# Cross-attention in two-step cycles of four runs on TensorE, PSUM banks in three pairs, exponential in two instructions

## The chip, the cores and the metric

The kernel runs on one core of a Trainium2 chip. The metric is device time in microseconds (us) of one execution, launch to end, as the median of several runs. Engines: PE is TensorE (matmul), ACT is ScalarE, DVE is VectorE, POOL is GpSimd, SP is SyncE, which here only issues DMAs. They run side by side, each in its own program order, and wait for each other by semaphores.

## The reference, cut to what matters

A decoder layer on x of shape (32, 56, 256): multi-query self-attention, then cross-attention to a context of shape (32, 1500, 256) with a mask, then a feed-forward part with quantised inputs and weights. The change touches the part after the self-attention:

```python
q = proj(layernorm(x), Wq, bq, 56)                     # 16 heads of 16
k = proj(ctx, Wk, bk, 1500); v = proj(ctx, Wv, bv, 1500)
scores = clip(q k^T / 4, -50, 50); scores = where(mask, scores, -50)
probs = softmax(scores)                                 # over 1500
x = x + layernorm(clip(rs, 0, .3) * ((probs v) Wo^T + bo)) * g + b
h = silu(bitlin(layernorm(x), gate_w)) * bitlin(layernorm(x), val_w)
x = x + bitlin(h, out_w)      # bitlin rounds its input to 127 steps of the row's maximum
```

## The kernel before, in words

The first block (up to about 349 us) does the self-attention; the change doesn't touch it. The second, `block_b`, does the rest and takes the batches in 16 pairs (i = 0 to 15). A batch's context is 1500 columns, loaded in three chunks of 500, so a pair has six chunks (c = 0 to 5), numbered x = 6i + c over the whole kernel. A chunk is four tiles of 125; two tiles are a twin, so a pair has 12 twins (t = 0 to 11), of which the first six are the first batch's.

What the engines do for it, with the four kinds of PE work by the letters that the text uses:

- SP loads chunk x + 3 into a ring of three buffers `raw` once POOL has read the one before it (line 1094).
- ACT copies it to `high` (fp32r, `split_high`, line 1199) and POOL subtracts to get `low` (`split_low`, line 1140), one instruction for each 128 rows, so two each.
- PE projects keys in two pieces, `piece` 0 and 1 (**K**, line 1451, 6 matmuls of 128x500 each), and values in two, `piece` 2 and 3 (**V**, line 1460, 12 matmuls of 128x256 each). All use the whole array. A piece goes to one of two PSUM banks `proj_ps[0]` and `proj_ps[1]`; keys are read out by ACT (`keys_out`, line 1204), values by DVE (`values_copy`, line 1251).
- PE makes the scores of a twin (**S**, line 1478): 16 fp32 matmuls (32 instructions) that use 32 rows of the array each, in four row groups; group r writes bank r of `score_ps`. ACT takes the exponential of all four banks in one instruction (`exp_twin`, line 1212), DVE limits and masks it in place, one instruction for each of the twin's two tiles (`limit`, line 1260).
- PE adds up probabilities times values and ones (**A**, `add_up`, line 1503): 32 fp32 matmuls (64 instructions) that use 32 columns of the array each, into `sum_ps`. After six twins DVE reads the sums (`read_sums`) and divides (`divide`).

The rest of the layer for pair i - 1, the tail, is spread over pair i by step numbers 0 to 12, one for each twin: two divides, 2 `project` (PE line 1520, then statistics on DVE), 3 `add_delta` (waits for POOL's `power`, line 1164, an inverse square root), 4 `quantise_rows`, 5 `rows_turned`, 6 and 7 the gate products and `gates`, 8 and 9 the value products, `values_` and `silu`, 10 `quantise_hidden`, 11 `hidden_turned`, 12 `finish`. The tail's products go through one bank, `side_ps`, guarded by `side_ready` and `side_read`.

With the four banks of `score_ps`, two of `proj_ps`, `sum_ps` and `side_ps` all eight PSUM banks are taken.

The order is written out by hand, one `body` for each engine. PE's repeats for each twin t: S(t), then K (t even) or V (t odd) of the next chunk, then A(t - 1). S(t) waits for the exponential of t - 1 (the four banks are free), K waits for the value copies and V for the key copies of the same bank, A waits for both `limit` of its twin. `exps` has two buffers. ACT: exponential of t, then for even t `keys_out` and `split_high` by turns. DVE: two `limit` of t - 1, then the tail step, and for odd t two `values_copy`. POOL, for each chunk c: two `split_low` (they wait for the two `split_high` of ACT), and behind them, in chunk 1, the two `power` and `add_bias` of the tail (lines 1166 to 1180). At the end of the kernel the tail of the last pair runs by itself, with idle matmuls (`spare`, line 907) between its steps.

Of the kernel before, what the change touches and what calls it, by code (L numbers as in the profile page):

```python
# [26 lines left out]
P = 128  # L27
# [34 lines left out]
GATES = (7, 8)  # L62
AFTER = (2, 5)
# [922 lines left out]
def block_b(nc, dram, out, keep, early):  # L986
# [3 lines left out]
    with ctx:  # L990
# [21 lines left out]
        exps = [sb(f"exps{n}", [TILE, 2, HR, QW]) for n in range(2)]  # L1012
# [26 lines left out]
        score_ps = ctx.enter_context(nc.psum_tensor("score_ps", [P, HR, 512], F32))  # L1039
        proj_ps = [ctx.enter_context(nc.psum_tensor(f"proj_ps{n}", [P, 512], F32)) for n in range(2)]  # L1040
# [43 lines left out]
        def up_ps(p, n):  # L1084

            return score_ps[0:ROWS, n - 2, :] if p == LAST else side_ps[0:ROWS, :]
# [108 lines left out]
        def _(act):  # L1195
# [5 lines left out]
            def keys_out(x, p, r):  # L1201

                act.wait_ge(piece_ready, 4 * x + p + 1)
                nc.scalar.activation(keys[r][:, p, :], proj_ps[p][:, 0:CHUNK], ACT.Identity,  # L1204
                                     bias=b_k[:, p:p + 1]).then_inc(keys_ready, 1)

            def exp_twin(i, t, warm):

                act.wait_ge(scores_ready, NT * i + t + 1)
                if warm:  # L1210
                    act.wait_ge(probs_used, NT * i + t - 1)
                nc.scalar.activation(exps[t % 2][:, :, :, :].rearrange("p h r n -> p r h n"),  # L1212
                                     score_ps[0:TILE, :, 0:2 * QW].rearrange("p r (h n) -> p r h n", h=2),
                                     ACT.Exp, scale=0.25).then_inc(exps_ready, 1)
# [6 lines left out]
            def body(i, first, last):  # L1221
                for t in range(NT):
                    c, half = divmod(t, 2)
                    x = PC * i + c
                    exp_twin(i, t, not first or t >= 2)
                    if half == 0:
                        for p in range(DC):
                            if not (last and c == PC - 1):
                                keys_out(x + 1, p, (c + 1) % 2)
                            if not (last and c >= PC - 2):  # L1230
                                split_high((c + 2) % 3, 2 * i + (c + 2) // 3 + 1, c % 2, p)
                    if not first and t in GATES:
                        gate_tanh(i - 1, GATES.index(t))

# [12 lines left out]
        def _(dve):  # L1247

            def values_copy(x, q, r):
                dve.wait_ge(piece_ready, 4 * x + q + 3)  # L1250
                nc.vector.tensor_copy(vals[r][:, 2 * q:2 * q + 2, :, 0:HD],  # L1251
                                      proj_ps[q][0:TILE, :].rearrange("p (k h d) -> p k h d", k=2, d=HD))\
                  .then_inc(vals_ready, 1)

            def limit(i, t, half):

                dve.wait_ge(exps_ready, NT * i + t + 1)
                tile = exps[t % 2][:, half, :, :].rearrange("p r n -> p (r n)")
# [135 lines left out]

            TAIL = 2 + 1 + 2 + 2 + 3 + 1 + 2 + 2 + 4 + 3 + 1 + 1

            def body(i, first, last):
                tail = {} if first else tail_steps(i - 1, False)
                for t in range(NT):
                    c, half = divmod(t, 2)  # L1400
                    for k in range(2):
                        if t:
                            limit(i, t - 1, k)
                        elif not first:
                            limit(i - 1, NT - 1, k)
                    if t == 1 and not first:
                        read_sums(i - 1, 1)
                    if t == BN + 1:
                        read_sums(i, 0)
                    if t in tail and t not in AFTER:  # L1410
                        tail[t]()
                    if last and t == BN + 3:
                        divide(i, 0)
                    for q in range(2) if half == 1 and not (last and c == PC - 1) else ():
                        if q == 1 and t in tail and t in AFTER:
                            tail[t]()
                        values_copy(PC * i + c + 1, q, (c + 1) % 2)
# [252 lines left out]
```

## Time and profile before

| | |
|---|---|
| median of 3 runs (lowest, highest) | 1390.54 us (1390.42, 1393.0) |
| the profiled execution | 1393.26 us, its span 1391.5 us |
| busy PE, PE weight load | 1369.0, 1171.2 us |
| busy DVE, ACT, POOL | 997.8, 720.7, 518.4 us |
| granted PE clock | 0.998 of full speed |

The span is from the first to the last instruction. Busy time is the union of an engine's instructions. A matmul's end is modelled, and the matmuls overlap in the array, so a PE that is busy all the time may still lose time between them: the distance between the starts of two matmuls is what shows it. In the views a group of like instructions is merged into one row: its start, the time from the first start to the last end, and its count.

### The profile page before, as it was taken

Reading aid. Unit: us, or ns where it says so; the run is one execution under the profiler, and the core shown is the slowest. Engines: PE = TensorE matmul, PEld = TensorE weight load, DVE = VectorE, ACT = ScalarE, POOL = GpSimd, SP = SyncE. Lnnn points to the kernel's source line nnn. Section 1 sums busy time; section 2 is a strip of 40 time slices with the busy share of each in tenths; the row PEclk is TensorE's granted clock in tenths of the full one; section 3 lists DMA queues with packets and bytes.
Section 4 is the critical chain, followed back from the end, with each engine's and each line's share of the span. In section 5 each row is a group of like instructions: output and inputs, shape, how many; then the busy total and the mean of one; then the engine's idle time right before and its main releaser. Section 6 shows DMA issues by size and latency. Waiting matters only on the chain.

```text
span 1391.5 us, 55868 instructions
## 1 busy us (share of the span) xinstructions
PE 1369.0 (98%) x25409; PEld 1171.2 (84%) x25409; DVE 997.8 (72%) x1821; ACT 720.7 (52%) x943; POOL 518.4 (37%) x494
## 2 busy tenths in 40 slices
PE   8999999999999999999999999999999999999997
PEld 6788888886888888888888888888888888888884
DVE  5788788785356867777676867677776868677766
ACT  3555454543555555555555555555554555555550
POOL 4656666651324233333323332433333242333310
PEclk9999999999999999999999999999999999999999
DMA  7010001010411211121202121121212122111100
GB/s 193 1 36 2 31 1 32 2 52 1 129 52 48 64 48 50 47 65 33 70 31 78 51 62 50 47 64 33 65 32 80 33 64 65 48 51 47 51 3 8
DMA packets 38957, 66.81 MB, mean 48 GB/s; under 512 B 3749, under 2 KB 36962, under 8 KB 38722
## 3 DMA queue, kind: packets, MB, share of 16 engines
q1 hardware_dynamic: 38722, 63.24, 15.4%
q8 instruction: 201, 3.29, 1.0%
q14 instruction: 34, 0.28, 0.1%
HBM read 61.40 MB, written 1.84 MB: 45 GB/s over the span
## 4 chain that ended last, share of the span: by engine, by line
PE 72%; DVE 2%; issue 0%; POOL 0%; DVEq 0%
PE proj_ps L1460 20%; PE proj_ps L1451 20%; PE score_ps L1478 15%; PE sum_ps L1503 13%; PE side_ps L1538 2%; PE side_ps L1552 1%; PE side_ps L1520 1%; PE side_ps L1545 1%; DVE amax L1338 0%; DVE hidden L1360 0%; DVE sig L1370 0%; DVE hidden L1371 0%; PE side_ps L1527 0%; DVE exps L1260 0%; DVE totals L1282 0%
## 5 line engine op out<-in xcount | busy, mean ns | idle before, releaser
L1212 ACT ACTIVATE exps<-score_ps 125x1792 f32<-125x1792 f32 x192 | 320.8, 1671 | 430.7 <-PE score_ps L1478 430.7
L1260 DVE TENSOR_SCALAR exps<-exps,top 125x896 f32<-125x896 f32 x384 | 289.0, 795 | 21.8 <-ACT exps L1212 17.5
L1478 PE MATMUL score_ps<-spread,keys 32*125 32x112 f32 x6144 | 219.0, 279 | 0.0
L1251 DVE COPY vals<-proj_ps 125x512 f32<-125x512 f32 x192 | 129.5, 688 | 115.6 <-PE proj_ps L1460 113.3
L1503 PEld LDWEIGHTS sum_ps<-exps,vals 125*32 125x32 f32 x12288 | 163.0, 110 | 47.1 <-issue 34.2
L1478 PEld LDWEIGHTS score_ps<-spread,keys 32*125 32x125 f32 x6144 | 184.8, 183 | 15.4 <-issue 0.3
L1503 PE MATMUL sum_ps<-exps,vals 125*32 125x56 f32 x12288 | 191.5, 215 | 0.0
L1140 POOL TENSOR_TENSOR low<-raw_early,high 128x500 fp32r<-128x500 f32 x64 | 84.4, 1323 | 217.8 <-PE proj_ps L1451 217.1
L1140 POOL TENSOR_TENSOR low_early<-raw_early,high_early 128x500 fp32r<-128x500 f32 x62 | 90.3, 1475 | 167.7 <-PE proj_ps L1451 167.7
L1204 ACT ACTIVATE keys<-proj_ps,b_k 128x500 f32<-128x500 f32 x192 | 130.0, 677 | 23.6 <-PE proj_ps L1451 19.8
L326 POOL TENSOR_TENSOR swapped<-swapped,sin 128x448 f32<-128x448 f32 (+1 forms) x72 | 85.6, 1192 | 79.4 <-ACT swapped L597 78.5
L737 PE MATMUL unit_ps<-xnT,w_q 128*128 128x224 f32 x512 | 107.8, 356 | 2.4 <-issue 1.8
L737 PEld LDWEIGHTS unit_ps<-xnT,w_q 128*128 128x128 f32 x512 | 92.6, 190 | 3.9 <-issue 2.1
L1140 POOL TENSOR_TENSOR low_early<-raw,high_early 128x500 fp32r<-128x500 f32 x32 | 40.6, 1274 | 129.1 <-PE proj_ps L1451 129.1
L1140 POOL TENSOR_TENSOR low<-raw,high 128x500 fp32r<-128x500 f32 x32 | 40.1, 1254 | 121.8 <-issue 113.7
L1460 PE MATMUL proj_ps<-w_h,high 128*125 128x256 f32 x384 | 82.7, 296 | 0.0
L1460 PE MATMUL proj_ps<-w_h,high_early 128*125 128x256 f32 x384 | 82.1, 295 | 0.0
L340 POOL TENSOR_TENSOR qT<-qT,swapped 128x448 f32<-128x448 f32 x56 | 76.5, 1376 | 2.2
L596 ACT COPY swapped<-unit_ps 64x448 f32<-64x448 f32 (+1 forms) x72 | 36.7, 510 | 77.5 <-PE unit_ps L737 59.5
L1460 PE MATMUL proj_ps<-w_l,high 128*125 128x256 f32 x384 | 76.7, 281 | 0.0
L1460 PE MATMUL proj_ps<-w_h,low 128*125 128x256 f32 x384 | 76.6, 281 | 0.0
L1460 PE MATMUL proj_ps<-w_h,low_early 128*125 128x256 f32 x384 | 76.5, 280 | 0.0
(186 smaller groups left out, 2742.7 us busy)
## 6 DMA issues: line engine op xcount, KB each, us to landing
raw_early<-in_ctxT SPq DMA_DIRECT2D x64, 500.0 KB, 4.1
raw<-in_ctxT SPq DMA_DIRECT2D x32, 500.0 KB, 3.5
w_q<-in_attn_Wq SPq DMA_DIRECT2D x4, 512.0 KB, 8.5
out<-y_out SPq DMA_DIRECT2D x16, 112.0 KB, 2.3
rows<-in_x SPq DMA_DIRECT2D x1, 1344.0 KB, 17.8
raw_early<-in_attn_Wo SPq DMA_DIRECT2D x1, 1024.0 KB, 18.0
raw_early<-in_ffn_gate_wT SPq DMA_DIRECT2D x1, 1024.0 KB, 5.3
raw_early<-in_ffn_val_wT SPq DMA_DIRECT2D x1, 1024.0 KB, 4.9
```

What stands on the lines that cost most here:

```text
L326: nc.gpsimd.tensor_tensor(swapped[r % 4][:, 0:w].rearrange("p (n s) -> p n s", s=S), swapped[r % 4][:, 0:w].rearrange("p (n s) -> p n s", ...
L340: nc.gpsimd.tensor_tensor(dst, dst, swapped[r % 4][:, :].rearrange("p (h b s) -> p h b s", h=2, s=S), ALU.add).then_inc(turned_ready, 1)
L737: ins = nc.tensor.matmul(to[:, h * GR:(h + 1) * GR].rearrange("p (b s) -> p b s", s=S), w_q[:, c, at:at + DH], xnT[g % 2][:, c, :, 0:S], s ...
L1140: nc.gpsimd.tensor_tensor(low[r][:, k, :], raw[ring][:, k, :], high[r][:, k, :].bitcast(F32), ALU.subtract).then_inc(low_ready, 1)
L1204: nc.scalar.activation(keys[r][:, p, :], proj_ps[p][:, 0:CHUNK], ACT.Identity, bias=b_k[:, p:p + 1]).then_inc(keys_ready, 1)
L1212: nc.scalar.activation(exps[t % 2][:, :, :, :].rearrange("p h r n -> p r h n"), score_ps[0:TILE, :, 0:2 * QW].rearrange("p r (h n) -> p r ...
L1251: nc.vector.tensor_copy(vals[r][:, 2 * q:2 * q + 2, :, 0:HD], proj_ps[q][0:TILE, :].rearrange("p (k h d) -> p k h d", k=2, d=HD))\
L1260: nc.vector.tensor_scalar(tile, tile, LIMIT_LO, top[:, n, at:at + 1], ALU.max, ALU.min)\
L1451: ins = nc.tensor.matmul(proj_ps[p][:, 0:CHUNK], w[:, 0, k, p * P:(p + 1) * P], part[r][:, k, :], start=(n == 0 and k == 0), stop=(n == 2 ...
L1460: ins = nc.tensor.matmul(proj_ps[p - 2][0:TILE, q * D:(q + 1) * D], part[r][:, k, at:at + TILE], w[:, 1, k, :], start=(n == 0 and k == 0), ...
L1478: ins = nc.tensor.matmul(score_ps[0:TILE, r, to:to + HE * S], keys[c % 2][32 * r:32 * r + 32, k, (at + half) * TILE:(at + half + 1) * TILE ...
L1503: ins = nc.tensor.matmul(sum_ps[32 * h:32 * h + VW, g, :], value_and_ones(c % 2, at + half, HJ * g + h), exps[t % 2][:, half, r, col:col + S],
```

## The change

Only `block_b` changes.

- PSUM: instead of four banks for scores and two for pieces there are three pairs of banks: `strip_ps` (two banks, scores of row groups 2 and 3 always) and `pair_ps[0]`, `pair_ps[1]`, which take turns: one holds the scores of row groups 0 and 1, the other the pieces.
- The exponential of a twin is two instructions of half the size: first over `strip_ps`, then over the pair. `exps_ready` counts both. `exps` has three buffers.
- PE's order is written for cycles m = 0 to 5 of a pair, with the even twin e = 2m and the odd one o = 2m + 1: S(e), A(e - 2), A(e - 1), S(o), tail step e, K, tail step o, V. So every kind of work follows itself twice.
- S(o) waits for the first half of the exponential of e, and for both value copies of the chunk (`vals_ready`), since its pair held the pieces of the cycle before. The next S(e) waits for both halves of the exponential of o. K waits for both halves of e's.
- ACT: exponential of e, of o, and then both `keys_out` and `split_high`. The two tanh of the tail move to m = 3 and m = 4.
- DVE: two `limit` of e, tail step e, two `limit` of o, tail step o, two `values_copy`. The tail steps 0 and 10 stand ahead of the `limit` of e.
- POOL and SP are unchanged.

```diff
+TWINS = NT // 2
+SLOTS = 3
-        score_ps = ...psum_tensor("score_ps", [P, HR, 512], F32)
-        proj_ps = [...psum_tensor(f"proj_ps{n}", [P, 512], F32) for n in range(2)]
+        strip_ps = ...psum_tensor("strip_ps", [P, HR // 2, 512], F32)
+        pair_ps = [...psum_tensor(f"pair_ps{n}", [P, 2, 512], F32) for n in range(2)]
+        def score_bank(t, r):
+            return pair_ps[(t // 2 + t) % 2][0:TILE, r, :] if r < HR // 2 else strip_ps[0:TILE, r - HR // 2, :]
+        def piece_bank(x, p):
+            return pair_ps[(x + 1) % 2][:, p % 2, :]
...
 exp_twin(i, t, warm):
                 act.wait_ge(scores_ready, NT * i + t + 1)
                 if warm:
-                    act.wait_ge(probs_used, NT * i + t - 1)
-                nc.scalar.activation(exps[t % 2]..., score_ps[0:TILE, :, 0:2 * QW]..., ACT.Exp, scale=0.25)
-                    .then_inc(exps_ready, 1)
+                    act.wait_ge(probs_used, NT * i + t - SLOTS + 1)
+                for at, banks in ((HR // 2, strip_ps), (0, pair_ps[(t // 2 + t) % 2])):
+                    nc.scalar.activation(exps[t % SLOTS][:, :, at:at + HR // 2, :]..., banks[0:TILE, :, 0:2 * QW]...,
+                        ACT.Exp, scale=0.25).then_inc(exps_ready, 1)
 ACT body:
+                for m in range(TWINS):
+                    exp_twin(i, 2 * m, ...)
+                    if not first and m == 4:
+                        gate_tanh(i - 1, 1)
+                    exp_twin(i, 2 * m + 1, ...)
+                    for p in range(DC):
+                        keys_out(x + 1, p, (m + 1) % 2)
+                        split_high((m + 2) % 3, ..., m % 2, p)
+                    if not first and m == 3:
+                        gate_tanh(i - 1, 0)
 DVE body:
+            AHEAD = (0, 10)
+                for m in range(TWINS):
+                    e, o = 2 * m, 2 * m + 1
+                    if e in AHEAD and e in tail:
+                        tail[e]()
+                    for k in range(2):
+                        limit(i, e, k)
+                    if e == 0 and not first:
+                        read_sums(i - 1, 1)
+                    if e == BN:
+                        read_sums(i, 0)
+                    if e in tail and e not in AHEAD:
+                        tail[e]()
+                    for k in range(2):
+                        limit(i, o, k)
+                    if o in tail:
+                        tail[o]()
+                    for q in range(2) if not (last and m == PC - 1) else ():
+                        values_copy(PC * i + m + 1, q, (m + 1) % 2)
 piece(x, p, r):
-                    pe.wait_ge(vals_ready, 2 * x + p - 1)
+                    pe.wait_ge(exps_ready, 2 * (2 * x - 1))
 scores(i, t):
-                if warm:
-                    pe.wait_ge(exps_ready, NT * i + t)
+                if t % 2:
+                    pe.wait_ge(exps_ready, 2 * (NT * i + t) - 1)
+                    pe.wait_ge(vals_ready, 2 * (PC * i + c) + 2)
+                elif warm:
+                    pe.wait_ge(exps_ready, 2 * (NT * i + t))
 PE body:
+                for m in range(TWINS):
+                    e, o = 2 * m, 2 * m + 1
+                    scores(i, e, not first or e >= 1)
+                    for n in (e - 2, e - 1):
+                        add_up(i, n, ...)          # of pair i - 1 where n < 0
+                    scores(i, o)
+                    if e in tail:
+                        tail[e]()
+                    piece(x, 0, r); piece(x, 1, r)
+                    if o in tail:
+                        tail[o]()
+                    piece(x, 2, r); piece(x, 3, r)
+                    # the last cycle: no pieces, but
+                    #   pe.wait_ge(exps_ready, 2 * (NT * PAIRS - 1)); spare(3); add_up(i, e, True)
+                    if o == NT - 1 and not first:
+                        tail[NT]()
```

## Rows read from the trace of the kernel before

**Rows 1.** The page: busy us of each engine, share of the span, instructions.

```profile
PE 1369.0 (98%) x25409; PEld 1171.2 (84%) x25409; DVE 997.8 (72%) x1821; ACT 720.7 (52%) x943; POOL 518.4 (37%) x494
```

**Rows 2.** PE, timeline: start, us, operation. A, S (then V), A, project, A.

```profile
923.37 0.99 PE L1503 MATMUL sum_ps<-exps,vals 125*32 125x56 f32 x64
924.30 1.14 PE L1478 MATMUL score_ps<-spread,keys 32*125 32x112 f32 x32
...
928.40 0.99 PE L1503 MATMUL sum_ps<-exps,vals 125*32 125x56 f32 x64
...
933.21 1.03 PE L1520 MATMUL side_ps<-w_xo,heads 128*112 128x256 f32 x4
...
934.17 0.99 PE L1503 MATMUL sum_ps<-exps,vals 125*32 125x56 f32 x64
```

**Rows 3.** PE, what is left of the A group of 923.37 in two later windows.

```profile
923.59 0.77 PE L1503 MATMUL sum_ps<-exps,vals 125*32 125x56 f32 x48
...
923.79 0.58 PE L1503 MATMUL sum_ps<-exps,vals 125*32 125x56 f32 x32
```

**Rows 4.** PE where the block starts: first matmuls of K, V, S, K, S.

```profile
348.92 0.69 PE L1451 MATMUL proj_ps<-high_early,w_h 128*128 128x500 f32 x2 [0.30 <-PEq L108]
...
351.72 0.40 PE L1460 MATMUL proj_ps<-w_h,high_early 128*125 128x256 f32 x2
...
354.64 1.14 PE L1478 MATMUL score_ps<-spread,keys 32*125 32x112 f32 x32
355.71 0.72 PE L1451 MATMUL proj_ps<-high,w_h 128*128 128x500 f32 x2
...
358.62 1.14 PE L1478 MATMUL score_ps<-spread,keys 32*125 32x112 f32 x32
```

**Rows 5.** ACT: two lines (fastest/median/slowest ns), then timeline after the S of 354.64.

```profile
L1212 ACT ACTIVATE exps<-score_ps x192: 1665/1671/1677, 355.8 to 1355.7; 125x1792 f32<-125x1792 f32 x192
...
L1218 ACT ACTIVATE sig<-gate x32: 619/628/634, 452.1 to 1378.2; 112x512 f32<-112x512 f32 x32
...
355.85 1.67 ACT L1212 ACTIVATE exps<-score_ps 125x1792 f32<-125x1792 f32 x1 [3.25 <-PE score_ps L1478]
...
358.73 0.68 ACT L1204 ACTIVATE keys<-proj_ps,b_k 128x500 f32<-128x500 f32 x1
```

**Rows 6.** The power line (fastest/median/slowest ns), then timeline about one: ACT, POOL, DVE.

```profile
L1164 POOL TENSOR_TENSOR rstd_b<-var_eps_b,minus_half_b x32: 582/655/1170, 429.8 to 1372.8; 112x1 f32<-112x1 f32 x32
...
932.65 0.61 ACT L1199 CAST high<-raw_early 128x500 fp32r<-128x500 f32 x1
...
933.39 2.53 POOL L1140 TENSOR_TENSOR low<-raw_early,high 128x500 fp32r<-128x500 f32 x2 [6.72 <-PE proj_ps L1451]
...
937.43 0.48 DVE L1314 SCALAR_TENSOR_TENSOR x<-delta,rstd_b,rows 112x256 f32<-112x256 f32 x1
...
939.41 1.28 DVE L1251 COPY vals<-proj_ps 125x512 f32<-125x512 f32 x2
```

**Rows 7.** DVE against POOL: two lines (fastest/median/slowest ns), then one meeting in the timeline.

```profile
L1260 DVE TENSOR_SCALAR exps<-exps,top x384: 673/681/1685, 357.5 to 1362.2; 125x896 f32<-125x896 f32 x192
...
L477 DVE TENSOR_TENSOR probs<-probs,sums x16: 1092/1829/1835, 41.8 to 328.5; 128x896 f32<-128x896 f32 x16
...
965.54 1.68 DVE L1260 TENSOR_SCALAR exps<-exps,top 125x896 f32<-125x896 f32 x1
...
965.25 1.48 POOL L1140 TENSOR_TENSOR low_early<-raw_early,high_early 128x500 fp32r<-128x500 f32 x1 [6.75 <-PE proj_ps L1451]
```

**Rows 8.** DVE timeline: hidden quantised, then limits; and a value product, two silu, limits.

```profile
909.33 1.22 DVE L1338 TENSOR_REDUCE amax<-hidden 112x1 f32<-112x1024 f32 x1
...
912.49 1.56 DVE L1260 TENSOR_SCALAR exps<-exps,top 125x896 f32<-125x896 f32 x1
...
962.58 0.75 DVE L1360 SCALAR_TENSOR_TENSOR hidden<-side_ps,dequant,val_b 112x512 f32<-112x512 f32 x1 [0.68 <-PE side_ps L1538]
...
964.93 2.28 DVE L1260 TENSOR_SCALAR exps<-exps,top 125x896 f32<-125x896 f32 x2
```

More of the change, by code:

```diff
@@ L1010, in block_b @@
         vals = [sb(f"vals{n}", [TILE, CT, XH, VW]) for n in range(2)]
-        exps = [sb(f"exps{n}", [TILE, 2, HR, QW]) for n in range(2)]
+        exps = [sb(f"exps{n}", [TILE, 2, HR, QW]) for n in range(SLOTS)]
         sums = sb("sums_b", [P, 2, HG // 2, S])
@@ L1037, in block_b @@
         y_out = sb("y_out", [ROWS, D])
-        score_ps = ctx.enter_context(nc.psum_tensor("score_ps", [P, HR, 512], F32))
-        proj_ps = [ctx.enter_context(nc.psum_tensor(f"proj_ps{n}", [P, 512], F32)) for n in range(2)]
+        strip_ps = ctx.enter_context(nc.psum_tensor("strip_ps", [P, HR // 2, 512], F32))
+        pair_ps = [ctx.enter_context(nc.psum_tensor(f"pair_ps{n}", [P, 2, 512], F32)) for n in range(2)]
         sum_ps = ctx.enter_context(nc.psum_tensor("sum_ps", [P, HG, S], F32))
@@ L1221, in body @@
             def body(i, first, last):
[L1222 to L1233, printed above, removed]
+                for m in range(TWINS):
+                    x = PC * i + m
+                    exp_twin(i, 2 * m, not first or 2 * m >= SLOTS)
+                    if not first and m == 4:
+                        gate_tanh(i - 1, 1)
+                    exp_twin(i, 2 * m + 1, not first or 2 * m + 1 >= SLOTS)
+                    for p in range(DC):
+                        if not (last and m == PC - 1):
+                            keys_out(x + 1, p, (m + 1) % 2)
+                        if not (last and m >= PC - 2):
+                            split_high((m + 2) % 3, 2 * i + (m + 2) // 3 + 1, m % 2, p)
+                    if not first and m == 3:
+                        gate_tanh(i - 1, 0)
             for k in range(DC):
@@ L1398, in body @@
                 tail = {} if first else tail_steps(i - 1, False)
-                for t in range(NT):
-                    c, half = divmod(t, 2)
+                for m in range(TWINS):
+                    e, o = 2 * m, 2 * m + 1
+                    if e in AHEAD and e in tail:
+                        tail[e]()
                     for k in range(2):
[L1402 to L1406, printed above, removed]
+                        limit(i, e, k)
+                    if e == 0 and not first:
                         read_sums(i - 1, 1)
-                    if t == BN + 1:
+                    if e == BN:
                         read_sums(i, 0)
-                    if t in tail and t not in AFTER:
-                        tail[t]()
-                    if last and t == BN + 3:
-                        divide(i, 0)
[L1414 to L1417, printed above, removed]
-                    if half == 0 and t in tail and t in AFTER:
-                        tail[t]()
+                    if e in tail and e not in AHEAD:
[4 more added lines that the diff above has]
+                        tail[o]()
+                    if last and o == BN + 3:
+                        divide(i, 0)
+                    for q in range(2) if not (last and m == PC - 1) else ():
+                        values_copy(PC * i + m + 1, q, (m + 1) % 2)
                 if not first:
@@ L1429, in _ @@
             body(LAST, False, True)
-            for half in range(2):
-                limit(LAST, NT - 1, half)
             read_sums(LAST, 1)
@@ L1463, in piece, with scores @@
                 ins.then_inc(piece_ready, 1)
-            def scores(i, t, warm):
+            def scores(i, t, warm=True):
                 c, at = t // 2, 2 * (t % 2)
@@ L1504, in add_up @@
                                 sum_ps[32 * h:32 * h + VW, g, :], value_and_ones(c % 2, at + half, HJ * g + h),
-                                exps[t % 2][:, half, r, col:col + S],
+                                exps[t % SLOTS][:, half, r, col:col + S],
                                 start=(t % BN == 0 and half == 0 and g == 0),
```

61 lines of the change are left out of this document (29 added, 32 removed).

## The prediction, written before the changed kernel was run

> **What bounds the kernel now.** I read the page's first part [rows 1]: PE is busy for 98% of the span, DVE for 72%, ACT for 52%. A full PE can be full of work or of change-overs, since its matmuls overlap in the records, so I went on to PE's timeline and read the distances between starts. One round of two twins is A, S, V, A, S, K. The distances [rows 2, 4]: A to S 0.93 or 0.92 (923.37 to 924.30), S to the next kind 1.07 (354.64 to 355.71), V to A 3.03 (924.30 + 1.07 to 928.40), K to its successor 2.91 (355.71 to 358.62). Sum 0.92 + 1.07 + 3.03 + 0.92 + 1.07 + 2.91 = 9.92 to 9.93 us, six times for each of 16 pairs.
>
> How much is work and how much is change-over? Inside one A, 16 instructions go by in 0.20 us (923.59 to 923.79) [rows 3], so 64 want 0.79, but the group takes 0.92: 0.02 is lost on entry (the first 16 take 0.22) and 0.11 on leaving. K from 348.92 runs straight on into V at 351.72: 2.80 [rows 4]; K followed by S takes 2.91. V that follows K takes 2.92 (351.72 to 354.64), V that follows S 3.03. So a change between the three forms of the array (whole, 32-row groups for S, 32-column groups for A) costs 0.1 to 0.2 us, and K to V, which keeps the form, nothing.
>
> **PE's new order, steady state.** Per cycle: S(e), A, A, S(o), K, V. Each distance from the rows above:
> - S(e), entered from V: that sequence stands in the trace, V at 351.72, S at 354.64, next kind at 355.71. I take 1.07. It is followed by A, which is nowhere in the trace.
> - first A 0.79 + 0.02 = 0.81, second A 0.79 + 0.11 = 0.90;
> - S(o) 1.07; K after S and before V 2.91 - 0.09 = 2.82; V after K 2.92.
>
> Sum 1.07 + 0.81 + 0.90 + 1.07 + 2.82 + 2.92 = 9.59, against 9.92: 0.33 less. The bounds of the unseen change-over S to A: if S leaves for nothing it gains another 0.1; if it costs what A to S costs, some 0.08 more on the entry of A. I take the middle, since each kind leaves at about 0.1 (K, V and A) and A enters at 0.02 after K or V. The last cycle of all has no pieces, so 95 x 0.33 = 31.4 us, with ends 95 x 0.43 = 41 and 95 x 0.25 = 24. I round the cycle to two places; by a mean of many distances it may be 0.32, so I carry **31**.
>
> The Trainium skill (TensorEngine Tiling (Array Packing), Key Properties) says that changing the tiling mode drains TensorE. By it every change of form costs, the unseen S to A too. By that rule alone 6 changes of form per two twins become 4, and two change-overs of 0.1 to 0.2 us in 95 rounds are 19 to 38 us, about the same sum; it speaks against the free end.
>
> **The exponential in two.** 1792 elements take 1.671, the tanh of 512 takes 0.628 [rows 5]. The slope is 0.815 ns an element, so a half of 896 takes 0.94; ACT's instructions, back to back, overlap by up to 0.1; both take 1.8, 0.1 to 0.2 more for each of 192 twins. In a cycle, with S(e) at 0: S ends in ACT 1.21 later (354.64 to 355.85) [rows 4, 5], the strip is read by 2.15, the pair by 3.0. S(o) wants the strip at 2.78, K wants both at 3.85. Exponential of o 3.99 to 5.8; the next S wants it at 9.6. Hidden by PE's two A, for nothing. At an upper bound of 1.67 for each half it would be 25% late and cost up to 1 us a cycle, but no row has an ACT instruction whose time doesn't shrink with its size.
>
> **The waits in a cycle without a tail.** S(o) waits for value copies of the cycle before. V ends at 0, DVE has copied by about 1.0, PE wants it at 2.78: free. Key copies: K's second piece can be copied 3.02 after K starts (355.71 to 358.73), so at 6.9, used at 9.6. The third buffer of `exps` makes the exponential of o wait for A(e - 2) only, over at 1.9. All free. SP's loads follow `low`, which is two cycles ahead of its use; POOL's own order is unchanged. So in pair 0 all 0.33 are kept.
>
> **With the tail, cycle 1: the power step is late.** This is the edit that I charge. In a pair with a tail, POOL's `power` stands behind the two `split_low` of chunk 1, these wait for ACT's `split_high`, and ACT now does both of them behind the exponential of o, not of e. Before, `low` ended at 935.92, the copies of values stood 3.5 us behind, and PE never waited [rows 6]. Now, with S(2) at 0:
> - S(3) at 2.78. `project` follows, 0.87 long (933.21 to 934.17 less the 0.09 for leaving) [rows 2], K at 4.72, S(4) at 9.59 + 0.87 = 10.46, S(5) at 13.24.
> - ACT: exponential of 3 from 3.99 to 5.8; the first key copy when piece 0 is done, at 6.3; `split_high` 6.85 to 7.46; second key copy 7.63, second `split_high` 8.21 to 8.81 (0.68 for a key copy [rows 5], 0.61 for a split [rows 6], each begun 0.1 before the one ahead of it has ended).
> - POOL: starts 0.13 behind a `split_high` (932.65 + 0.61 to 933.39), two of 1.26 (2.53 for both): 7.6 to 8.85 and 8.94 to 10.2. Then `power`: 0.58 to 1.17 [rows 6]. The slow ones met `limit`; here DVE has run dry and waits, so I take 0.6: done at 10.85.
> - DVE: both `limit` of 3 are over by 7.6. Then `add_delta` waits for `power`. Behind it on DVE stand both `values_copy`, and for these waits S(5), the new wait of this change, with all of PE behind it. From `x` to the first value copy 1.98 (937.43 to 939.41), both 1.28 [rows 6]. So 10.95 + 1.98 + 1.28 = 14.2, and 0.1 to PE: 14.3.
>
> PE wants S(5) at 13.24 and gets it at 14.3: **1.1 us of waiting per pair**, 15 pairs, 16.5 us. Bounds: a slow power 1.17 gives 1.7 (25 us); `split_high` half a us earlier gives 0.6 (9 us); if POOL were free of it, 0.
>
> **Cycles 4 and 5.** DVE is densest here: value product to limits 2.35 (962.58 to 964.93) twice, quantised hidden 3.16 (909.33 to 912.49) [rows 8]. In cycle 4: limits of 8 from 3.05, `values_`, `silu` to 6.8, limits of 9 of which one meets POOL's `low` of 7.1 to 8.4, then 2.35 again and 1.3 of copies: 12.9. S(11) wants them at 9.59 + 0.66 (two gate-size products) + 2.78 = 13.0. Just free. In cycle 5 the quantiser stands ahead of the limits, they end about 8.3 or, with one meeting, 9.3, `hidden_turned` 9.9, and `down` on PE wants it at 9.9: I take 0.1 a pair, 1.5 us.
>
> **The end.** In the last pair both limits of 11 stand ahead of `hidden_turned`, where before they stood behind `finish`. Two of 0.60 to 0.68 [rows 7] delay `down` by 1.3, of which what A(11) then needn't wait for comes back. 0.7 us, between 0 and 2.
>
> **Sum.** 31 - 16.5 - 1.5 - 0.7 = 12.3, and 0.3 off for the start of pairs 0 and 15: **12 us**. From the profiled 1393.26 (span 1391.5 and 1.8 around it) this gives 1381.3. The median of the runs is 2.7 below that execution, so 1390.54 - 12 = **1378.5 us**.
>
> **Rivals.**
> 1. *The power step hides.* If `split_high` comes earlier or POOL's order is not what decides, PE never waits: 1390.5 - 30 = 1361. For it: DVE is idle 28% of the span. Against: in the list above each step has a row, and it needs 1.1 us.
> 2. *S to A is dear, or the cycle gains less* (entry and exit as A to S, plus 1.7 for the wait): 24 - 25 - 2: 1390. Within a measurement of no change. For it: the sequence is not in the trace. Against: K and V both enter A at 0.02.
> 3. *Slower: DVE and POOL meet in cycles 4 and 5.* A limit that starts inside POOL's `low` takes 1.68, not 0.68: 965.54 began 0.29 behind one of 1.48, and stood until it was over [rows 7]. `low` now comes when exponentials of o are limited. DVE has 0.1 us left before PE there, so each further meeting is a wait of PE by 1.0. One in each of the two cycles is 2 x 15 = 30 us: 1378.5 + 30 = 1408; one in only one cycle, 1393.5. It decides from 0.8 us a pair (12/15). For it: the margins. Against: I have laid one meeting in each already, and POOL's work in a cycle is only 2.5 of 9.6 us.
>
> The self-attention's product with two SBUF operands takes 1.83 in the median and 1.09 at best [rows 7]; the `silu` have two such operands too and show 0.69 without POOL. The Trainium skill (SBUF — State Buffer, Who interferes with whom and the port notes before it) says that VectorE with two SBUF inputs is locked out while GpSimd reads SBUF. By it the four silu instructions join in rival 3, at up to 0.74 each; I raise that rival's chance for it.
>
> **Chances.** Forecast 0.57 (own range 1371 to 1386), rival 1 0.12, rival 2 0.13, rival 3 0.18. Faster by over 0.2% (2.8 us, about what can be told from no change): 0.57 + 0.12 + a third of rival 2 = 0.73; slower: 0.14 of rival 3; the rest, 0.13, the same. Range for 8 in 10: it leaves out most of rival 1 and the two-cycle end of rival 3: 1364 to 1394.
>
> **What would show it.** After the change, PE's distances S to A, A to A 0.81, A to S 0.90, K to V 2.82, S(e) to S(e) 9.6 in pair 0. In pairs 1 to 15 the wait view has PE's S line waiting for `vals` on DVE, some 15 times about 1.1, and DVE's x3 line waiting for POOL's power. A pair of the middle takes about 0.8 us less (12/15). ACT busy rises by about 192 x 0.2 = 38 us at most. I am wrong if the pair's S(5) does not wait, if `low` runs earlier than 7.6 behind S(2), or if PE waits at S(11) or `down` for more than 0.3 us.

## The result and the profile after

The changed kernel takes **1457.89 us** (median of 4 runs, 1452.58 to 1462.12) against 1391.70 for the kernel before on the same chip (1390.42 to 1393.0): a ratio of 1.0475, 95% interval 1.0454 to 1.0496. Predicted were 1378.5 us and a range up to 1394. The profiled execution took 1460.63 us, with a span of 1458.8.

From the page after: busy time, two lines of the exponential, the instruction queue, and the chain of waits by engine.

```profile
PE 1375.1 (94%) x25406; PEld 1191.7 (82%) x25406; DVE 990.0 (68%) x1821; ACT 733.9 (50%) x1135; POOL 512.6 (35%) x494
...
q8 instruction: 201, 3.29, 0.9%
...
PE 57%; issue 12%; DVE 6%; POOL 1%; ACT 0%; DVEq 0%
...
L1223 ACT ACTIVATE exps<-strip_ps 125x896 f32<-125x896 f32 x192 | 176.4, 919 | 458.1 <-PE strip_ps L1492 458.1
...
L1223 ACT ACTIVATE exps<-pair_ps 125x896 f32<-125x896 f32 x192 | 175.2, 912 | 0.0
```

PE is busy for 94% instead of 98% [rows 1]: it has holes. "issue", time in which the profile shows nothing that is waited for, has 12% of the chain, and 0% in the page before. That share mixes two things. Two runs of the next section tell them apart: e1, which has PE's holes but not the late power step, and e10, which has the late power step and next to no holes:

```profile
PE 70%; issue 4%; DVE 2%; ACT 0%; POOL 0%; DVEq 0%
...
PE 56%; issue 11%; DVE 7%; POOL 1%; ACT 0%; DVEq 0%
```

So some 4 of the 12 points are the holes, and the rest is DVE's wait for the power step, for which the profile names no releaser (the last line below). PE's wait view after (us in total, times, longest), and one line of DVE's:

```profile
PE sum_ps L1517 <- issue: 15.9, 10, 2.6
PE pair_ps L1492 <- issue: 15.1, 13, 2.2
PE pair_ps L1492 <- DVE vals L1264: 14.0, 14, 1.3
PE strip_ps L1492 <- issue: 11.1, 10, 1.9
...
DVE x L1327 <- issue: 49.7, 15, 4.2
```

Of PE's lines only the third is a wait that the prediction has. DVE's line is its other half: `x` stands for about 3 us or more in 15 pairs until POOL's `power` is done; in e9, which differs from e10 only in the place of that step, it waits for 0.1 or less. A cycle with that wait, PE's timeline from S(4) to the next S:

```profile
842.75 0.36 PE L1492 MATMUL pair_ps<-spread,keys 32*125 32x112 f32 x2
...
843.82 1.78 PE L1517 MATMUL sum_ps<-exps,vals 125*32 125x56 f32 x128
846.56 0.36 PE L1492 MATMUL pair_ps<-spread,keys 32*125 32x112 f32 x2 [0.96 <-DVE vals L1264]
...
847.63 0.72 PE L1462 MATMUL pair_ps<-high,w_h 128*128 128x500 f32 x2
...
850.45 0.27 PE L1541 MATMUL side_ps<-ident_h,xq 112*128 112x112 bf16 x2
850.54 0.48 PE L1471 MATMUL pair_ps<-w_h,high 128*125 128x256 f32 x2
...
853.55 0.36 PE L1492 MATMUL pair_ps<-spread,keys 32*125 32x112 f32 x2
```

S to A 1.07, S to K 1.07, K 2.82, V 3.01 behind one short step of the tail: as the prediction put them. A to S is 2.74 here, and 1.71 where nothing is waited for (595.21 to 596.92, below; predicted 0.81 + 0.90). The lost time is elsewhere, in the middle of groups. Two stretches of the same timeline:

```profile
595.21 1.78 PE L1517 MATMUL sum_ps<-exps,vals 125*32 125x56 f32 x128
596.92 0.36 PE L1492 MATMUL pair_ps<-spread,keys 32*125 32x112 f32 x2
...
597.13 0.27 PE L1492 MATMUL strip_ps<-spread,keys 32*125 32x112 f32 x1
598.85 0.25 PE L1492 MATMUL strip_ps<-spread,keys 32*125 32x112 f32 x1 [1.45 <-issue]
```

```profile
730.43 1.68 PE L1517 MATMUL sum_ps<-exps,vals 125*32 125x56 f32 x119
734.38 0.34 PE L1517 MATMUL sum_ps<-exps,vals 125*32 125x56 f32 x9 [2.27 <-issue]
734.65 0.36 PE L1492 MATMUL pair_ps<-spread,keys 32*125 32x112 f32 x2
```

119 matmuls of an A run, PE stands for 2.27 us, and the last 9 follow. No semaphore lies between them. The places of such gaps in the instruction stream can be counted. PE's records (matmuls, weight loads, separate waits) are numbered in order of time. The block has 36 gaps of over 0.45 us between two weight loads of one line with no wait for a semaphore before them, and all 36 stand where the number is 193 or 194 modulo 256. They hold 49.8 us. The kernel before has none. Gaps down to 0.2 us and those between two lines counted too, 42 stand at these places, with 57 us in all; the longest of the added ones is 2.7 us at 665.81, between an A and an S.

The page says what there are 256 of. q8 moves 3.29 MB in 201 packets, 16.4 KB each. (The Trainium skill, Vector Engine (DVE) Microarchitecture Reference, Why there are multiple struct shapes, gives every instruction 64 bytes; by it a packet is, as an estimate, 256 instructions. The runs below agree: 3792 more instructions made 15 more packets and 0.25 MB.) One packet falls into the stretch before the second gap, in the DMA view of 731.6 to 735:

```profile
q8 instruction: 1, 0.02, 1.7%
```

It starts at 732.13 and has landed at 733.07; the A goes on 1.31 later. Of the other gaps too each ends 1.1 to 1.6 us behind a landing. So the theory, **F**, by which the experiments were laid out: PE's instructions come in packets of 256, the next one is fetched only when an old one is used up, and from there to its first instruction about 3.4 us go by (1 to the start, 1 for the packet, 1.35 to its use). Matmuls of K and V are long, 24 and 48 instructions in 2.8 and 2.9 us. S has 64 instructions in 1.07 us, A 128 in 0.86. Before, no two fast groups but one A and one S stood together, and a packet lasted 5.1 us or more (the last one 3.8). Now S A A S puts 384 instructions into 3.85 us.

The traces bear out the last two terms and not the first. At the 36 gaps 2.2 to 3.0 us lie between the start of a fetch and the first new instruction. But the fetch starts at no fixed time: from 0.3 us ahead of the first instruction of the packet in use to 2.4 behind it, once 3.2. And 3.4 us is no sharp limit. The block has 175 packets; counted from packet end to packet end in PE's records, 62 of them were used up in less, and of these 41 ended in a gap of over 0.2 us and 20 in none. In the 41 the fetch had started 1.2 us behind the first instruction of the packet in use, in the 20 about 1.0 us ahead of it (medians). So a packet that is used up fast runs dry when its successor is asked for late; what decides on that stays open.

Behind some gaps the granted clock falls. Windows around the second one (PE, PEld, DVE, ACT, POOL busy, PEclk, DMA):

```profile
732.00:735.00 3.00, 0.73 (x31) 0.54 (x25) 1.28 (x2) 0.81 (x2) 0.00 (x0) 1.00 0.03 9
735.30:738.70 3.40, 3.40 (x27) 2.57 (x20) 1.32 (x2) 1.73 (x2) 0.00 (x0) 0.50 0.02 5
```

For 3.41 us PE has half its clock (1.2 of 2.4 GHz) and makes the work of 1.7. There are 13 such stretches, 47.8 us in all, each begun 0.3 to 1.6 us behind the end of a standstill of PE of 0.8 to 2.8 us; one of them lies ahead of the block. Before there were 2.

Over the block (first to last S) the time goes from 1000.8 to 1068.3 us, 67.5 more: gaps 57, half clock some 22 (half of the 44.4 us of 12 stretches), waits at S(5) 14, less 31 for the order. That leaves some 5 unplaced.

### The profile page after: what moved, and what is told of

It is laid out like the page before. It is cut to its first block, busy times and chain, and to the rows that moved or that the text cites. A ratio compares the mean times of both kernels' runs of the same rounds, so it can differ in the third digit from the quotient of the medians.

```text
span 1458.8 us, 56148 instructions
## 1 busy us (share of the span) xinstructions
PE 1375.1 (94%) x25406; PEld 1191.7 (82%) x25406; DVE 990.0 (68%) x1821; ACT 733.9 (50%) x1135; POOL 512.6 (35%) x494
## 3 DMA queue, kind: packets, MB, share of 16 engines
q8 instruction: 201, 3.29, 0.9%
## 4 chain that ended last, share of the span: by engine, by line
PE 57%; issue 12%; DVE 6%; POOL 1%; ACT 0%; DVEq 0%
PE pair_ps L1462 17%; PE pair_ps L1471 16%; PE pair_ps L1492 10%; PE sum_ps L1517 8%; PE side_ps L1552 2%; PE strip_ps L1492 2%; DVE vals L1264 1%; PE side_ps L1566 1%; DVE exps L1273 1%; POOL spread L1156 1%; DVE x L1327 0%; DVE stats_b L1310 0%; PE side_ps L1559 0%; DVE spread L1332 0%; DVE delta L1323 0%
## 5 line engine op out<-in xcount | busy, mean ns | idle before, releaser
L1223 ACT ACTIVATE exps<-strip_ps 125x896 f32<-125x896 f32 x192 | 176.4, 919 | 458.1 <-PE strip_ps L1492 458.1
L1492 PE MATMUL pair_ps<-spread,keys 32*125 32x112 f32 x3072 | 224.1, 281 | 30.2 <-issue 15.1
L1492 PE MATMUL strip_ps<-spread,keys 32*125 32x112 f32 x3072 | 224.3, 282 | 11.1 <-issue 11.1
L1492 PEld LDWEIGHTS pair_ps<-spread,keys 32*125 32x125 f32 x3072 | 186.6, 185 | 53.8 <-issue 24.7
L1492 PEld LDWEIGHTS strip_ps<-spread,keys 32*125 32x125 f32 x3072 | 186.4, 185 | 16.2 <-issue 16.2
L1264 DVE COPY vals<-pair_ps 125x512 f32<-125x512 f32 x192 | 128.3, 687 | 88.7 <-PE pair_ps L1471 88.3
L1223 ACT ACTIVATE exps<-pair_ps 125x896 f32<-125x896 f32 x192 | 175.2, 912 | 0.0
L1214 ACT ACTIVATE keys<-pair_ps,b_k 128x500 f32<-128x500 f32 x192 | 130.7, 680 | 50.4 <-PE pair_ps L1462 46.0
L1150 POOL TENSOR_TENSOR low<-raw,high 128x500 fp32r<-128x500 f32 x32 | 43.5, 1371 | 137.0 <-issue 121.4
L1471 PE MATMUL pair_ps<-w_h,high 128*125 128x256 f32 x384 | 80.5, 291 | 0.2 <-issue 0.2
L1471 PE MATMUL pair_ps<-w_h,high_early 128*125 128x256 f32 x384 | 80.4, 291 | 0.0
L340 POOL TENSOR_TENSOR qT<-qT,swapped 128x448 f32<-128x448 f32 x56 | 76.5, 1376 | 2.2
```

The costliest lines, as they stand in the source:

```text
L340: nc.gpsimd.tensor_tensor(dst, dst, swapped[r % 4][:, :].rearrange("p (h b s) -> p h b s", h=2, s=S), ALU.add).then_inc(turned_ready, 1)
L1150: nc.gpsimd.tensor_tensor(low[r][:, k, :], raw[ring][:, k, :], high[r][:, k, :].bitcast(F32), ALU.subtract).then_inc(low_ready, 1)
L1214: nc.scalar.activation(keys[r][:, p, :], piece_bank(x, p)[:, 0:CHUNK], ACT.Identity, bias=b_k[:, p:p + 1]).then_inc(keys_ready, 1)
L1223: nc.scalar.activation(exps[t % SLOTS][:, :, at:at + HR // 2, :].rearrange("p h r n -> p r h n"), banks[0:TILE, :, 0:2 * QW].rearrange("p ...
L1471: ins = nc.tensor.matmul(piece_bank(x, p)[0:TILE, q * D:(q + 1) * D], part[r][:, k, at:at + TILE], w[:, 1, k, :], start=(n == 0 and k == 0 ...
L1492: ins = nc.tensor.matmul(score_bank(t, r)[:, to:to + HE * S], keys[c % 2][32 * r:32 * r + 32, k, (at + half) * TILE:(at + half + 1) * TILE ...
```

## The experiments

Ratios are against the kernel before on the same chip. The gaps are those of over 0.45 us between weight loads of one line at packet ends, the half-clock stretches those behind the first S.

| run | us | ratio, 95% interval | gaps, us | half-clock stretches |
|---|---|---|---|---|
| after | 1457.89 | 1.0475, 1.0454 to 1.0496 | 36, 49.8 | 12 |
| e1_power | 1444.23 | 1.0371, 1.0316 to 1.0426 | 37, 53.5 | 10 |
| e2_split_only | 1416.38 | 1.0182, 1.0165 to 1.0199 | 0 | 1 |
| e4_split_power | 1407.84 | 1.0118, 1.0103 to 1.0133 | 0 | 1 |
| e3_two_a | 1396.67 | 1.0039, 1.0026 to 1.0052 | 15, 15.3 | 1 |
| e5_aligned | 1457.03 | 1.0462, 1.0438 to 1.0486 | 11, 8.7 | 3 |
| e7_aligned_no_power | 1460.91 | 1.0495, 1.0479 to 1.0511 | 9, 6.4 | 3 |
| e6_misaligned | 1620.47 | 1.1639, 1.1610 to 1.1667 | 80, 135.3 | 25 |
| e8_steered | 1379.48 | 0.9912, 0.9896 to 0.9929 | 2, 1.9 | 0 |
| e11_before_waits | 1392.02 | 1.0007, 0.9997 to 1.0016 | 0 | 0 |
| e10_steered | 1388.27 | 0.9977, 0.9968 to 0.9987 | 6, 2.7 | 1 |
| **e9_steered_power** | **1371.28** | **0.9850, 0.9834 to 0.9866** | 4, 1.9 | 0 |

**The power step first (e1).** POOL does the power of a tail ahead of the two `split_low` of chunk 1.

```diff
+                    if c == 1 and not first:
+                        power(2 * (i - 1))
                     if not (last and c >= PC - 2):
...
                     if c == 1 and not first:
-                        power(2 * (i - 1))
                         power(2 * (i - 1) + 1)
```

> The changed kernel with POOL's first power of the tail ahead of the two split_low of chunk 1, nothing else. Theory F (instruction supply: PE's instructions come in packets of 256, and a stretch in which 256 of them are used up in less than some 3.4 us runs dry): the wait of S(5) for the value copies goes (15 x 1.1 = 16 us, a few us more if half-clock stretches go with it), the gaps in the middle of S and A groups stay at 40 to 60 us. Time 1430 to 1442 against 1458. Rival P (the power wait starts everything, the other gaps and the lost clock follow from it): the gaps go too, 1360 to 1390. Rival G (the gaps are waits for the new banks or the half exponentials that the profile does not show): as F, 1430 to 1442.

1444.23, 2 us above F's range, and its 4 runs spread over 20 us. The wait at S(5) is gone, and the time fell by 13.7 us, near the 16.5 that the prediction charges, but 53.5 us of gaps stay: theory P, that this wait is the loss, falls.

**The burst cut in two (e2, e4).** PE's order becomes S(e), A(e-2), S(o), K, A(e-1), V; e4 has the power step of e1 as well.

```diff
-                    for n in (e - 2, e - 1):
-                        add_up(i, n, ...)
+                    older(e - 2)
                     scores(i, o)
...
                         piece(x, 1, r)
+                    older(e - 1)
```

> The changed kernel with its banks, its half exponentials and its two-twin cycle, but the two A taken apart: S(e), A(e-2), S(o), K, A(e-1), V on PE, and the reading of the sums on DVE behind the limits of o. Six changes of the array's form per cycle again, as in the kernel before, so a steady cycle of 9.93. Theory F: no stretch of 256 instructions is short now, the gaps inside S and A groups go from about 53 us to under 8, and nearly all half-clock stretches with them: 1391 plus about 0.8 x 15 for the power wait, 1395 to 1412. Rival G (banks, half exponentials): the gaps stay, 1391 + 50 + 12 + clock, 1450 or more. Rival P: the power wait is still there, so gaps and clock loss stay, 1450 or more.

> Both edits of the two kernels above on the changed kernel: the two A taken apart, and the first power ahead of split_low. Theory F: neither gaps nor power wait are left, six changes of form, so the time of the kernel before within 4 us: 1387 to 1396. Rival G: 1430 or more. Rival P: 1391 as well.

All gaps go, and with them 41.5 us (1457.89 to 1416.38); the new banks and the halved exponential are still there, so theory G, that these two make the gaps, falls. Both runs stay above what was expected (1395 to 1412, 1387 to 1396), for a reason that F has nothing to do with. PE, then ACT, of e2:

```profile
704.13 0.36 PE L1492 MATMUL pair_ps<-spread,keys 32*125 32x112 f32 x2
...
705.20 0.99 PE L1517 MATMUL sum_ps<-exps,vals 125*32 125x56 f32 x64
706.30 0.36 PE L1492 MATMUL pair_ps<-spread,keys 32*125 32x112 f32 x2
```

```profile
705.33 0.92 ACT L1223 ACTIVATE exps<-strip_ps 125x896 f32<-125x896 f32 x1 [3.95 <-PE strip_ps L1492]
```

With one A between them, S(o) must wait for the first exponential, which ends at 706.25: A to S takes 1.10 instead of 0.92, 0.18 x 95 = 17 us. Two A between S(e) and S(o) hide it. That is what the cut costs, and why e4 is no faster than before.

**Two A alone (e3).** Banks, exponential and cycle of before, a third buffer of `exps`, and both A in every second step: S K A A S V.

```diff
-                    if t:
-                        add_up(i, t - 1, not first or t - 1 >= BN)
+                    for n in (t - 2, t - 1) if t % 2 == 0 else ():
+                        add_up(i, n, not first or n >= BN)
```

> The kernel before with its own banks, its one exponential and its pieces where they were, with a third exps buffer, and the A of two twins one behind the other: S(e), K, A, A, S(o), V. Five changes of form instead of six, so about 0.2 x 95 = 19 us less work for PE. Theory F: two A are 256 instructions in 1.7 us, PE runs dry at packet boundaries here too, gaps of 30 to 60 us and some ten half-clock stretches appear: 1400 to 1440. Rival G and rival P (no new banks, no half exponentials, no power wait here): no gaps, 1368 to 1376.

1396.67, slower than before by 0.4% although it saves a change-over. That is below F's range (1400 to 1440), with half of the gaps that it named or less, and far above the 1368 to 1376 of G and P. The gaps are back, in a kernel that has neither the new banks nor the halved exponential. Its burst A A S has 320 instructions, fewer than S A A S, and its loss is a third. PE's wait view:

```profile
PE score_ps L1478 <- issue: 9.9, 11, 1.4
```

**Moving the packet ends (e5, e6, e7).** If it only matters where a packet ends, instructions that do nothing must be able to help or harm. Waits on a semaphore that has had its value since the start were put between the matmuls of K and V: two of them in a row add one instruction. Their numbers per cycle were chosen so that a packet should end 170 instructions behind the start of S(e) (e5, e7), or 20 and 276 behind it (e6). e5 and e6 have e1's power step, e7 hasn't.

```diff
+            def pad():
+                n, j = slots
+                slots[1] += 1
+                for _ in range(2 * (n * (j + 1) // 32 - n * j // 32)):
+                    pe.wait_ge(setup_p, 3)
...
                         for k in range(DC):
+                            if n or k:
+                                pad()
                             ins = nc.tensor.matmul(...)
```

> The changed kernel with the first power ahead (as in e1_power), and with satisfied waits put between the matmuls of K and V, counted so that every cycle is two packets of 256 instructions and a packet ends 170 instructions behind the start of each S(e), that is in the middle of the first A: 3845 instructions more, the same matmuls in the same order. Theory F: no packet is used up in less than about 4 us, so there are no gaps and no half-clock stretches, while the 31 us of fewer form changes stay: 1360 to 1370, faster than the kernel before by 1.5% to 2.2%. Rival G (gaps come from banks or exponentials): as e1_power, 1435 to 1450. Rival I (it is the number of instructions, or each added one costs PE time): 1450 or more.

> The same as e5_aligned, with nearly the same number of satisfied waits (3995), but counted so that packets end 20 and 276 instructions behind the start of each S(e): a whole packet lies in S, A, A and is used up in 2.1 us. Theory F: a gap in every cycle at the end of that packet, 1.0 to 1.6 us each, 95 of them, and many half-clock stretches: 1480 to 1560. Rivals G and I: the same time as e5_aligned, within 5 us.

> The changed kernel with the waits of e5_aligned alone, POOL's order as in the change. Theory F: no gaps at packet ends, the wait of S(5) for the value copies stays with 1.1 us in each of 15 pairs: 16 to 20 us above e5_aligned, 1376 to 1388, so faster than the kernel before by 0.3% to 1.1%, about what the prediction said. Rival P (power wait sets off the rest): 1430 or more.

e6 against e5 is the plainest proof: 3995 and 3845 added instructions, which do nothing, differ in place, and lie 163 us apart. (The 150 more, at the 0.12 us found below, are 18 us at most.) G and I, which wanted e6 within 5 us of e5, fall for this difference. e6's wait view, and e5's:

```profile
PE sum_ps L1533 <- issue: 122.6, 80, 2.4
...
PE pair_ps L1487 <- issue: 5.8, 11, 1.1
```

At 1620.47 e6 is also 60 us above what F gave it, and it shows F's limit again: in each of its 95 cycles a packet is used up in 2.0 us, and 80 end in a gap, 15 in none. In the 80 the fetch starts 0.5 to 2.4 us behind the packet's own first instruction, in most of the 15 1.1 ahead of it. e5's 11 gaps are in V, at packet ends too, each 1.4 to 1.7 us behind a landing, though by PE's records the packets lasted 5.0 us; F has none there.

And e5 and e7 were 90 and 80 us slower than expected, as rival I (each added instruction costs time) had it for e5. I had taken the waits to be free. The timeline of e5, where K and V of one cycle start, and the next S:

```profile
622.78 0.72 PE L1476 MATMUL pair_ps<-high,w_h 128*128 128x500 f32 x2
...
625.62 0.40 PE L1487 MATMUL pair_ps<-w_h,high 128*125 128x256 f32 x2
...
631.39 0.36 PE L1508 MATMUL pair_ps<-spread,keys 32*125 32x112 f32 x2
```

K with 21 added instructions takes its 2.84, V with 47 takes 5.77, of which 0.23 is a gap at a packet end: 0.12 each. In most cycles V had 28 to 32 and took 3.4 to 3.9, again 0.12 each, instead of 2.94. So up to about 23 of them (2.8 / 0.12) should lie hidden beside a K or a V. e7 is only 3.9 us above e5, not 16 to 20: beside the longer V most of the wait at S(5) is gone (2.1 us in 6 pairs), so its time says nothing about theory P.

**Few waits, on e3 (e8).**

> The kernel of e3 (banks and exponential of before, a third buffer of exponentials, order S K A A S V) with 1248 added waits on PE that are satisfied since the start, up to 24 in a cycle, half of them between the matmuls of K and half between those of V, chosen so that the end of an instruction packet falls outside A A S where it can. e3 lost 16.7 us in 14 gaps at packet ends. Theory F (PE runs out of instructions where a packet is used up in less than about 3.4 us): most of these gaps go, some 8 us are left for want of room, the waits in K cost nothing (in e5 K stayed at 2.82) and those in V little while they are few (in e5, 20 in every V made it 3.70 instead of 2.92, 0.04 each; 600 of them here are up to 20 us if each costs that, 0 to 10 if the matmuls hide the first): 1380 to 1395. Rival W (each added wait takes PE's sequencer 0.125 us wherever it stands, and none of it is hidden): 1396.7 - 9 + 1248 x 0.04 to 0.125, 1437 or more. Rival G (the gaps have to do with the three forms of the array or with the waits of A, not with where the packets end): gaps stay, 1397 or more.

1379.48, 17.2 us less than e3 and 0.9% less than before, 0.5 below F's range. W (each wait costs wherever it stands) and G fall. With 12 added instructions in K and 12 in V no distance grew. (The expectation says that e5 had 20 in every V: it was 28 or more, 30 in the V of 3.70, which makes F's allowance for them too large.) Here too 3.4 us is no sharp limit: e8 still uses up 26 packets in less, and 1 of them ends in a gap of over 0.2 us.

**The changed kernel with waits spread (e9, e10), and the waits alone (e11).** 20 added instructions in each K and 20 in each V bring a cycle from 461 to 501, near 2 x 256, and its burst stays where it is against the packets.

```diff
+            def pad(x, j, slots):
+                n = PADS[x - 1] // 2 if x else 0        # 40 in all cycles but two with 36
+                for _ in range(2 * (n * (j + 1) // slots - n * j // slots)):
+                    pe.wait_ge(setup_p, 3)
...
+                            if n or k:
+                                pad(x, 5 * p + 2 * n + k - 1, 10)                # in K
...
+                                if q or n or k:
+                                    pad(x, 11 * (p - 2) + 6 * q + 2 * n + k - 1, 22)   # in V
```

> The kernel of e1 (the changed kernel with the first power ahead of the split_low of chunk 1) with 40 satisfied waits added in every cycle, 20 in K and 20 in V. They bring the instructions of a cycle from 461 to about 501, so that against packets of 256 the burst S A A S comes back to nearly the same place, with one packet end some 140 to 230 instructions behind the start of S(e) and none else in the burst. Unlike e5, whose waits stood by two thirds in V (28 of them, and V took 3.38 to 3.90 instead of 2.94), here neither K nor V has more waits than 0.125 us each would fill of its 2.82 or 2.92 us (22 or 23); 12 in each cost nothing in e8. Theory F (instruction supply is what the change lost its time to, the half-clock stretches come behind its gaps): e1's 1444 less 58 us of gaps and most of the 25 us of half clock that do not overlap them: 1362 to 1380, faster than before. Rival W (waits cost wherever they stand): as e5, 1440 to 1460. Rival G (the order S A A S itself loses the time, wherever packets end): 1430 or more.

> The changed kernel as it is, with the same 3792 added waits as e9 and the power step where the change left it. Theory F: e9 plus the wait for the value copies at S(5), 1.1 us in each of 15 pairs: 1378 to 1396, near the 1378.5 that the prediction gave. Rivals W and G: 1450 or more. Rival N (the wait at S(5) costs nothing once the gaps are gone, because the gaps had put PE and DVE out of step): the same as e9.

> The kernel before with the 40 satisfied waits of e9 in every cycle, 20 in K and 20 in V, and nothing else changed: what the waits do by themselves, where there is no gap at a packet end to take away. Theory F: nothing; 12 to 20 of them hide beside the matmuls of a K or a V (some cycles of e9 have a V of 3.1 instead of 3.02, and a gap of 0.1 to 0.4 in a cycle), and the packets of 256 are now used up in 4.6 to 5.2 us, still over 3.4: 1389 to 1402. Rival H (the waits speed PE up by themselves, by keeping its queue from running ahead, and e9 owes its time to that): 1375 or less. Rival W (each costs): 1400 plus 95 x 40 x 0.04 or more.

e9 takes 1371.28, e10 1388.27. The same instructions of work in the same order as in e1 and in the changed kernel, and 73.0 and 69.6 us less, by 3792 instructions that do nothing. In the kernel before they do nothing in the time either (1.0007), so they don't speed PE up by themselves (rival H). All three lie in F's ranges; G and W fall. The page of e9, and the wait at S(5) in e10:

```profile
PE 1343.3 (98%) x25406; PEld 1170.5 (85%) x25406; DVE 1005.1 (73%) x1821; ACT 733.4 (54%) x1135; POOL 533.3 (39%) x494
...
q8 instruction: 216, 3.54, 1.0%
```

```profile
PE pair_ps L1503 <- DVE vals L1264: 15.2, 16, 1.2
```

e9 is the fastest, 1.5% below the kernel before and 5.9% below the changed one.

## Why the prediction was wrong

**PE's new order, 9.59 a cycle: the distances right, the total not.** S to A 1.07, A A 1.71, S 1.07, K 2.82, V 2.92 (pair 0 of e9: 383.95 to 393.55, 9.60). The step that failed is the product "95 x 0.33 = 31.4 us". It takes PE to have its next instruction always at hand, since it always had in the trace of before. There was no term for instruction supply and no rival with one: with the gaps (57 us) and the half clock behind them (some 22) as a term, the sum 1378.5 + 79 is 1457.5, against 1457.89. That it comes so near is luck: e10, in which this term is nearly gone, shows 8.5 us more than the rest of the sum says (below). "So in pair 0 all 0.33 are kept" is refuted by the first pair: its cycles take 9.60, 9.60, 9.91 and 11.89 from S(2) on, the last two with gaps, and it has 59.83 from S to S where before had 58.67. What the trace of before could have told: 201 packets for 51,000 instructions, a packet used in 5.1 us or more, and that an A and an S go by at 0.007 and 0.017 us an instruction. It could not tell where PE runs dry; a range that knew of it would have been open at the top.

**The power step: right.** 1.1 us a pair, 16.5 us. The rows show gaps of 0.96 to 1.3 in 13 pairs of the changed kernel, DVE's x line waits in 15 pairs, and the pure price is e10 less e9: 17.0 us (rival N of e10 falls). In the changed kernel gaps at packet ends took the place of two of these waits: at 1323.19 S(5) comes behind a gap of 2.8 in its A and waits for nothing, at 1389.80 behind one of 0.9 and waits 0.1.

**The exponential in two: right.** 0.92 and 0.91 for a half (0.94 predicted), ACT busy 13.2 us more (at most 38 was said), and PE waits for it once in the changed kernel: 1.0 us at 357.51, in the very first cycle, which has no A between its two S. e2 shows what hid it: the two A.

**Cycles 4 and 5, 1.5 us, and the end, 0.7.** Up to 1422 us PE waits for nothing of DVE's in the block but the value copies, so rival 3 did not come: of the 384 `limit` 12 take over 1 us, where before it was 46, and the mean is 713 ns instead of 795. The `silu` did meet POOL's `low`: 12 of 32 take 0.86 to 0.87 and two 1.72 and 1.73, instead of 0.69, and PE did not feel it. Neither term is told apart from nothing.

**The sum without supply.** e10 is the changed kernel with its supply put nearly right: 3.5 us faster than before in the medians, where the prediction says 12. Of the 8.5 missing, some 5 are what is left of delays at packet ends in its trace; the tail steps, in their new places between other forms of the array, seem to cost more too (a pair of e9 is 61.6 to 62.4 from S to S, six cycles of 9.60 leave 4.0 to 4.8 for the tail, before 63.26 less six of 9.93 left 3.7), which no run takes apart. Rival 1 is e9 with the same shortfall: 1361 said, 1371 measured.

**Rival 2** (S to A dear) is refuted by 842.75 to 843.82: 1.07.

**What stays open.** Why a packet is asked for only when it is (at the gaps, 2.2 to 3.0 us ahead of its use), why that comes late at some packets that are used up in 2 us and early at others, and whether a gap alone, or the work before it too, brings the clock down: 36 gaps, 12 stretches. No run tells these apart. That the half clock follows from the gaps is shown only by its going and coming with them in the runs of the table.

## What to carry to other kernels

Before fast, small instructions are moved together, count them: in this kernel PE ran dry at 41 of the 62 packets whose 256 instructions, weight loads included, went by in less than 3.4 us, and at one of the 113 others. Long matmuls between them are cover for the supply as they are for waits; gaps labelled "issue" in the middle of a group, always at the same place modulo 256, are the sign. Where a burst can't be cut, its place against the packet ends can be moved with a few instructions that hide beside long matmuls.

## What the runs showed of the hardware

- PE's instruction stream arrives in packets of 16.4 KB for 256 instructions (201 packets; 216 with 3792 instructions more). At the 36 gaps of the changed kernel a fetch took 0.9 to 1.7 us, mostly about 1, and from its landing to the first new instruction 1.1 to 1.6 us went by.
- A packet used up fast ran dry or not by when the next fetch began: in e6, with 95 packets of 2.0 us each, 80 gaps with the fetch 0.5 to 2.4 us behind the packet's first instruction, and 15 packets without.
- A wait that is already satisfied takes 0.12 us of PE's sequencer as a separate instruction: 30 of them made a V of 3.70 us and 47 one of 5.77 (0.23 of it a gap), 20 were hidden in its 2.9 (e9, e11).
- The place of packet ends moved one kernel by 163 us (e5 to e6, of which 150 more waits can be 18), and it makes about 70 us between the changed kernel and e10.
- Behind some standstills of PE of 0.8 to 2.8 us the granted clock was 0.50 for 3.41 us (once for 6.83); e6, with 80 gaps, had 25 such stretches.
